# In step 7 the turn of the rows and six products move ahead of the turn of the sums; idle products in two early gaps

## The reference

```python
h = jnp.maximum(_layernorm(x, axis=-1), 0.0)
agg = jax.ops.segment_sum(edge_attr, receivers, num_segments=N_NODES)
x1 = jnp.concatenate([agg, h], axis=1)              # 6250 x 256
out = x + jax.nn.relu(x1 @ W1 + b1) @ W2 + b2        # 256 -> 512 -> 128
```

## Time and profile before

| | |
|---|---|
| timed runs, median of 3 | 202.59 us (202.53 to 202.75) |
| profiled execution, whole time | 202.15 us |
| its span | 198.4 us |
| TensorE busy | 188.5 us, 95% |
| VectorE, ScalarE, GpSimd busy | 135.4, 118.0, 84.4 us |
| DMA queue of the edges and rows | 61.66 MB, 87.9% of the 16 engines' span |
| mean over the span | 315 GB/s |

### The profile page before, as it was taken

The page is one execution under the profiler, slowest core; times in us unless marked ns, Lnnn a source line. Parts: engine busy times, 40 slices in busy tenths (PEclk is TensorE's granted clock), DMA queues, the critical chain, the costliest instruction groups (busy, mean ns, idle before and its releaser), DMA issues.

```text
span 198.4 us, 6644 instructions
## 1 busy us (share of the span) xinstructions
PE 188.5 (95%) x2426; PEld 154.4 (78%) x2426; DVE 135.4 (68%) x481; ACT 118.0 (59%) x244; POOL 84.4 (43%) x239
## 2 busy tenths in 40 slices
PE   7797899998998999999999999999999999999994
PEld 5585789785796788788888888787788887788794
DVE  2997774667837966966957957967958847834521
ACT  3454526543744856865855855866757756947650
POOL 6573202202670860841832832834814814806000
PEclk9999999999999999999999999999999999999999
DMA  5999999999999999999999999989899999401011
GB/s 203 386 375 377 362 377 373 378 375 373 377 375 376 375 380 384 390 377 378 371 317 380 382 337 374 380 311 368 266 324 375 339 380 382 162 3 56 0 55 41
DMA packets 44627, 62.46 MB, mean 315 GB/s; under 512 B 1822, under 2 KB 44300, under 8 KB 44594
## 3 DMA queue, kind: packets, MB, share of 16 engines
q1 hardware_dynamic: 44264, 61.66, 87.9%
q10 hardware_dynamic: 330, 0.36, 0.6%
HBM read 58.81 MB, written 3.20 MB: 313 GB/s over the span
## 4 chain that ended last, share of the span: by engine, by line
PE 77%; DMA 7%; DVE 3%; POOL 3%; issue 3%; SPq 2%; ACT 1%; DVEq 1%; POOLq 0%; ACTq 0%
PE bank L990 20%; PE bank L1091 14%; PE bank L1055 13%; PE bank L1059 13%; DMA edges<-in_edge_attr 6%; PE bank L1005 4%; PE bank L1030 3%; PE bank L1040 3%; PE bank L1099 3%; PE bank L1078 2%; PE bank L1014 2%; DMA xs<-in_dst 2%; POOL aggT L420 1%; DVE aggT L714 1%; SPq L323 1%
## 5 line engine op out<-in xcount | busy, mean ns | idle before, releaser
L420 POOL TENSOR_TENSOR aggT<-turned,aggT 128x32 f32 x120 | 31.0, 293 | 62.5 <-ACT turned L572 60.8
L990 PE MATMUL bank<-edges,onehot 128*32 128x128 f32 x1656 | 52.2, 275 | 2.1 <-DMA edges<-in_edge_attr 1.2
L990 PEld LDWEIGHTS bank<-edges,onehot 128*32 128x32 f32 x1656 | 43.1, 110 | 9.8 <-issue 6.2
L626 DVE TENSOR_TENSOR onehot<-relT,iota 128x384 f32<-128x384 f32 x69 | 36.0, 551 | 0.0
L714 DVE TENSOR_TENSOR aggT<-bank,aggT 128x32 f32 x157 | 20.8, 191 | 19.5 <-PE bank L1005 15.4
L513 ACT ACTIVATE w<-bank,bias_col 128x512 f32<-128x512 f32 x36 | 24.8, 689 | 10.7 <-PE bank L1059 5.1
L468 ACT ACTIVATE xn<-xs,shift,rstd 128x128 f32<-128x128 f32 (+1 forms) x49 | 21.4, 484 | 11.5 <-POOL shift L403 11.5
L718 DVE TENSOR_TENSOR hid_lo<-w,hid_hi 128x512 fp32r<-128x512 f32 x36 | 24.7, 686 | 3.6 <-ACT hid_hi L514 3.6
L670 DVE TENSOR_TENSOR agg_lo<-aggT,agg_hi 128x256 fp32r<-128x256 f32 (+1 forms) x25 | 10.5, 418 | 23.2 <-ACT agg_hi L490 23.2
L514 ACT ACTIVATE hid_hi<-bank,bias_col 128x512 fp32r<-128x512 f32 x36 | 24.6, 683 | 0.0
L395 POOL TENSOR_SCALAR var<-meanvar 128x2 f32<-128x2 f32 (+1 forms) x25 | 10.3, 412 | 29.3 <-DVE meanvar L646 27.8
(11 more groups left out here) (137 smaller groups left out, 335.5 us busy)
## 6 DMA issues: line engine op xcount, KB each, us to landing
edges<-in_edge_attr SPq DMA_DIRECT2D x69, 768.0 KB, 9.1
xs<-in_x SPq DMA_DIRECT2D x21, 128.0 KB, 9.7
out_rows<-xs SPq DMA_DIRECT2D x10, 256.0 KB
w<-in_L_gnn_W SPq DMA_DIRECT2D x3, 256.0 KB, 10.4
out_rows<-xs SPq DMA_DIRECT2D x4, 128.0 KB
xs<-in_x SPq DMA_DIRECT2D x1, 256.0 KB, 5.7
xs<-in_dst SPq DMA_DIRECT2D x1, 192.0 KB, 3.1
xs<-in_dst ACTq DMA_DIRECT2D x1, 192.0 KB, 3.2
```

Source lines behind the costliest of these rows:

```text
L420: nc.gpsimd.tensor_tensor(win, turned[:, at:at + W], win, ALU.add).then_inc(agg_added, 1)
L626: nc.vector.tensor_tensor(hot, of.unsqueeze(2).to_broadcast([p, n, W]), iota[0:p, 0:W].unsqueeze(1).to_broadcast([p, n, W]), ALU.is_equal) ...
L990: ins = nc.tensor.matmul(sums_ps[t * W:(t + 1) * W, cols], onehot[:, hots, e, :], edges[:, slot, e * F:(e + 1) * F], start=(g == 0), stop= ...
```

## The change

In the branch for odd steps from 5 on, groups up to `FIRST` (so steps 5 and 7) take a new order: the turn of the rows comes before the turn of the sums. In step 7 the six products with h of the first two quarters stand between the two turns, and `layer1_pair` then leaves them out. Those six wait for what all products with h waited for (`hidden_ready`, `hT_lo_ready` 7). From step 9 on the order is as before. `idle` takes its width from its target, and is called twice more: ten products of 128 columns in front of step 1's first round, and six behind its turn of the rows. Both write to `spare_ps`, the last quarter of the bank of the sums, which step 1 with its three rounds does not use.

```diff
+        spare_ps = sums_ps[:, 3 * F:4 * F]
...
-            def layer1_pair(n):
-
+            def products_h(n, t):
                 here = slice(start_of(n), start_of(n) + 2 * BLOCK)
+                for i, (wt, v) in enumerate(((w1_hi, hT_hi), (w1_hi, hT_lo), (w1_lo, hT_hi))):
+                    nc.tensor.matmul(hid_ps[t][:, :], wt[:, 1, t * P:(t + 1) * P], v[:, here], start=(i == 0), stop=False)
+
+            def layer1_pair_h(n, first, last):
+
                 pe.wait_ge(hidden_ready, n * HT)
                 pe.wait_ge(hT_lo_ready, blocks_of(n)[-1] + 1)
+                for t in range(first, last):
+                    products_h(n, t)
+
+            def layer1_pair(n):
+
+                if n > FIRST:
+                    pe.wait_ge(hidden_ready, n * HT)
+                    pe.wait_ge(hT_lo_ready, blocks_of(n)[-1] + 1)
                 for t in range(HT):
...
-                    for i, (wt, v) in enumerate(((w1_hi, hT_hi), (w1_hi, hT_lo), (w1_lo, hT_hi))):
-                        nc.tensor.matmul(hid_ps[t][:, :], wt[:, 1, to], v[:, here], start=(i == 0), stop=False)
+                    if n > FIRST or t >= 2:
+                        products_h(n, t)
...
             def idle(n, to):
+                cols = min(to.shape[1], 2 * P)
                 for _ in range(n):
-                    nc.tensor.matmul(to[:, 0:2 * P], warm[:, 0:P], warm, start=True, stop=True)
+                    nc.tensor.matmul(to[:, 0:cols], warm[:, 0:P], warm[:, 0:cols], start=True, stop=True)
...
             layer1_h(1, 1, 2, 4)
+            idle(10, spare_ps)
             for k in range(1, NB):
...
                     turn_x(2)
+                    idle(6, spare_ps)
                     pe.wait_ge(w1_ready, 2)
...
-                    turn_sums(k)
-                    turn_x(k + 1)
+                        turn_sums(k)
+                        turn_x(k + 1)
+                    else:
+                        turn_x(k + 1)
+                        if one == FIRST:
+                            layer1_pair_h(one, 0, 2)
+                        turn_sums(k)
```

More of the change, by code:

```diff
@@ L57, in graph_layer @@
     ROUNDS = [list(range(rounds_by(b - 1) if b else 0, rounds_by(b))) for b in range(NB)]
-    assert max(len(r) for r in ROUNDS) <= 4
+    assert max(len(r) for r in ROUNDS) <= 4 and len(ROUNDS[1]) == 3
     def chunks_of(r):
```

## The result

| | before | changed |
|---|---|---|
| median of 6 timed runs | 202.59 us (202.21 to 202.85) | 201.00 us (200.71 to 201.32) |
| profiled execution, whole time | 202.15 us | 200.71 us |
| its span | 198.35 us | 198.93 us |
| whole time less span | 3.80 us | 1.78 us |

The ratio is 0.9922, 95% interval 0.9909 to 0.9936: the changed kernel is faster by 1.6 us, four times what can be told from no change. I had forecast 202.8 us and no measurable change. Yet its span is longer than before. The whole difference, and more, lies outside the span, between the last instruction of the kernel and the end of the execution: behind that instruction the trace's last semaphore update comes 2.02 us sooner than before.

What follows compares the result with a forecast made beforehand. TensorE, busy 95% of the span, was taken as the bound. Terms -0.07 + 0.35 + 0 - 0.10 = +0.18 us, rounded to +0.2, on the 202.59 us median gave 202.8 us; range 202.3 to 203.1.

Steps and rivals of the forecast that it cites:

- the sum's last: Whole kernel: +0.2 us added to the profiled 202.15 us, with 3.75 around its span, giving 202.35 us.
- They gain nothing either: the clock is at 2.4 GHz here already: Sixteen idle products in step 1's gaps gain nothing, since the clock is at 2.4 GHz there already.
- Idle products' cost, nothing: Step 1: ten products take 0.55 to 1.1 us in a 0.89 us gap, six fit 1.10 us; no cost.
- Step 7: turn_x(8) waits for hT_lo, starting at 63.34; three transposes of sums then add 0.35 us; subtotal +0.28 us.
- Step 5: Swapped turns let the copy turned start 0.49 us earlier; 0 to -0.49 us arrives behind it, -0.10 taken.
- signs of being wrong: turn_x(8) before 62.8, a TensorE wait in step 8, or the early region to step 5 moving over 0.1 us.
- Both slacks are over 1.8 us ... so I price them at nothing: Behind step 7, hid_lo and xn come 1.0 to 1.3 us later, within their slacks: cost nothing.
- Rival 4: Step 8: GpSimd's additions slow beside builds, xn 9 comes late, turn_x(9) waits 1.0 us: 203.8 us; chance 6%.
- no TensorE wait after 64 us: Expected sign in the changed profile: TensorE's list of waits stays empty from 64 us on, as before.

Runs made afterwards that it cites:

- e1: Only the sixteen idle products added to the kernel before, orders of steps 5 and 7 unchanged: 200.39 us, ratio 0.9890.
- e2: The changed kernel without its sixteen idle products, so the new orders of steps 5 and 7 alone: 203.39 us, ratio 1.0037 to the kernel before.
- e3: The kernel before with sixteen products written into TensorE's branch that is never taken: 200.45 us, ratio 0.9898.
- e4: The kernel before with four products (eight instructions) in TensorE's branch that is never taken: 200.42 us, ratio 0.9899.
- e6: The changed kernel with hT_lo of block 7 made ahead of the additions of step 6 on VectorE: 199.35 us, ratio 0.9825 to the kernel before.
- e7: The changed kernel with step 5 in its old order, turn of the sums first: 201.18 us, ratio 0.9917 to the kernel before.
- e5: The changed kernel with VectorE's register load of step 8 moved ahead of agg_lo of block 7: 200.69 us, ratio 0.9889 to the kernel before.
- e10: The kernel before with 126 products (252 instructions) in TensorE's branch that is never taken: 202.96 us, one run.
- e9: The kernel before with one product (two instructions) in TensorE's branch that is never taken: 202.20 us, one run.

## Why the prediction was wrong, point by point

**The step that failed** is the sum's last: "The profiled execution has 202.15 us, 3.75 around its span, so it would be 202.35". I added my +0.2 to a time outside the span taken as fixed. It went from 3.80 to 1.78 us, -2.02, and this one term is larger than all I had worked out. e1 and e2 show that the idle products bring it and the new orders do not; e3 and e4 show that eight or 32 instructions more in TensorE's code bring it without being executed. I had priced the idle products by time in their gaps only, not by length of code. Why the length matters (a border between code blocks, by my reading) is not shown.

**"They gain nothing either: the clock is at 2.4 GHz here already"** was true of the profiled execution and not of all. In about one of three executions of kernels without them the clock fell and cost about 1 us (25 of 76). In the six runs behind the ratio this cannot have been much: they reach from 202.21 to 202.85.

**Idle products' cost, nothing: right.** TensorE at the start of the changed kernel, beside the earlier trace rows:

```profile
17.38 0.73 PE L1118 MATMUL bank<-xs 128*128 128x128 bf16 x10
18.04 0.86 PE L991 MATMUL bank<-edges,onehot 128*32 128x128 f32 x24
...
19.11 0.50 PE L1118 MATMUL bank<-xs 128*128 128x128 bf16 x6
20.76 0.36 PE L1041 MATMUL bank<-agg_hi,w_hi 128*128 128x256 f32 x1 [1.15 <-DVE agg_lo L671]
```

Ten take 0.73 us, within the 0.55 to 1.1 us I had set, and end at 18.11, ahead of the 18.40 at which the round had started before; the round now starts at 18.04. The six take 0.50 us. agg's products start at 20.76 against 20.73.

**Step 7: right.** turn_x(8) was held by hT_lo, 1.12 us, starting at 63.22 (forecast: 63.34 less 0.10). The turn of the sums followed 1.64 us later without a wait (forecast: 1.6), and step 8 started 0.16 us later (forecast: 0.18). e6 shows the reason by removing it.

**Step 5: right, its size at the upper end.** TensorE and the chain behind it, beside the earlier trace rows:

```profile
48.64 0.42 DVE L664 TENSOR_TENSOR hT_lo<-bank,hT_hi 128x256 fp32r<-128x256 f32 x1 [0.32 <-ACT hT_hi L476]
...
49.21 0.41 PE L1015 MATMUL bank<-ident,xn 128*128 128x128 f32 x2 [0.18 <-DVE hT_lo L664]
...
49.65 0.55 PE L1006 MATMUL bank<-ident,sums 128*128 128x128 f32 x3
...
50.23 0.49 ACT L573 ACTIVATE turned<-bank 128x384 f32<-128x384 f32 x1
...
50.43 0.50 PE L1041 MATMUL bank<-agg_hi,w_hi 128*128 128x512 f32 x1 [0.24 <-DVE agg_lo L671]
...
50.91 2.09 POOL L421 TENSOR_TENSOR aggT<-turned,aggT 128x32 f32 x6 [3.48 <-ACT turned L573]
...
58.38 0.42 DVE L671 TENSOR_TENSOR agg_lo<-aggT,agg_hi 128x256 fp32r<-128x256 f32 x1 [2.93 <-ACT agg_hi L491]
```

turn_x(6) starts at 49.21 (forecast: 49.40), the turn of the sums at its old 49.65, agg's products still at 50.43, turned at 50.23 (forecast: 50.24). Of the 0.49 us, 0.17 arrived at agg_lo of block 5 (58.80 against 58.97) and at hT_lo of block 7 (63.07 against 63.24), between the 0.10 I took and the 0.21 I allowed. The rest went where I had put it: the first six additions took 2.09 us instead of 1.75, beside VectorE's builds. One of my signs of being wrong did turn up, without consequence: in the changed profile several rounds before step 5 end over 0.1 us earlier (round 9 at 31.46 us instead of 31.68). But e7, whose start is the same, has 31.76, so this is spread between executions, and the third round of step 5, held by its load, ends at 49.03 in both main profiles.

**"Both slacks are over 1.8 us ... so I price them at nothing": wrong, by 0.44 us.** I followed hid_lo and xn to their use by TensorE only. A third line carries the same delay: turned, GpSimd's additions and its shift of the rows behind them, xn on ScalarE, agg_hi behind xn, agg_lo of block 7, VectorE's register load, the additions of step 8, the turn of the sums of step 9. xn did have its slack for turn_x(9), which came without a wait; it was agg_hi, next in ScalarE's order, that had none. e5 cuts the line at the load and the wait goes. Rival 4 had the stretching of the additions beside VectorE's work (12 took 5.05 us instead of 3.83), but looked for the wait at turn_x(9). And the sign "no TensorE wait after 64 us" failed with it. With 0.16 and 0.44 the span should be 0.6 us longer; its median is 199.2 us over the changed kernel's executions, against 198.5 over the 28 executions of before whose clock did not fall, so 0.7. e2, with the time outside the span as before, has a ratio of 1.0037, 0.75 us more, with 0.04 to 0.70% as its interval.

**The sum as it was**: +0.16 (step 7, with step 5's 0.17 in it) +0.44 (step 9) -2.02 (outside the span) = -1.42 us, against -1.44 in the two profiled executions and -1.59 in the medians. The 0.15 us left in the medians lies within the spread of single runs (0.6 us in each kernel).

The best version that the experiments give is e6: 199.35 us, 3.5 us below the median of its group's runs of before and 3.1 below those of them whose clock did not fall (202.5). Of these 3.1 us about 0.8 is the shorter span (197.6 against 198.4) and the rest lies outside it: the new order pays once hT_lo no longer holds it, but less than the length of the code does.

## What to carry to other kernels

Before work is moved in front of a wait, look up what it waits for itself, and where on the other engine that is made: here both stood behind the same twelve additions, and the new order paid only once that engine's order followed. A delay of a step goes down every line that leaves it, so list them all up to where each one meets the bounding engine again, in-order neighbours included. And compare the time outside the span of two kernels before a difference under 1% is explained by their schedules; a few unexecuted instructions are a cheap test of it.

## What the runs showed of the hardware that was not expected

- Length of code that is not executed changes the time: with 0 or 2 instructions more in an untaken branch 3.5 to 4.3 us pass outside the span, with 8, 32 or 224 more 1.8 us, with 252 more 3.3 us.
- The same kernel on one core can lose its full clock in some executions and not in others: 16 of 44 executions of the kernel before did. In the profiles of e2 and e10 it fell behind an early stretch in which TensorE waited 2.06 us for agg_lo; e3 and e9 waited as long and kept it. The cost is about 1.1 us (in e1's group the runs of before have a median of 203.4 us with the fall and 202.3 without). With 16 idle products in that stretch it was none of 36.
- GpSimd's additions of 128 x 32 take 0.21 us each undisturbed, and 0.60 us on average in the stretch of the changed kernel where VectorE builds and hid_lo lie beside them (six in 3.62 us). The six before those ran beside VectorE's statistics of the rows and were not slowed (1.26 us).
